# Filter spectrum computed behind the experts, input stage moved ahead of it, three early value chunks, query stacks issued from ScalarE

## The reference

```python
x = x + xattn0(layernorm(x), ctx)          # 16 heads, 1601 keys
x = x + ffn0(layernorm(x))                 # 8 experts, top 2 of each token
x = x + xattn1(layernorm(x), ctx, ...)     # top-32 attention, film, s4d, MLP
x = x + ffn1(layernorm(x))                 # attention with gated values

def s4d(x, ...):                           # inside xattn1
    powers = jnp.exp(dtA[:, :, None] * jnp.arange(L))
    K = 2.0 * jnp.einsum('dn,dnl->dl', dC, powers).real
    Kf = jnp.fft.rfft(K, n=n, axis=-1)     # the filter's spectrum: once
    xf = jnp.fft.rfft(x, n=n, axis=1)
    y = jnp.fft.irfft(xf * Kf.T[None], n=n, axis=1)[:, :L]
    return y + x * D_skip
```

## Time and profile before

| | |
|---|---|
| Median of 3 runs | 2865.64 us (2865.42 to 2866.55) |
| The profiled execution's own time | 2862.61 us |
| Its span | 2860.8 us |
| TensorE busy | 2277.7 us (80%) |
| VectorE, ScalarE, GpSimd busy | 1464.1, 1456.8, 917.3 us |
| Mean granted TensorE clock | 0.895 of 2.4 GHz |

### The profile page before, as it was taken

One profiled execution on the slowest core, in us unless ns is written; L12 is line 12 of the kernel. 1 busy time (PEld: TensorE's weight loads), 2 busy tenths in 40 slices (PEclk: granted clock), 3 DMA queues, 4 the chain that ended last, 5 costly groups with the idle time before them and its releaser, 6 DMA issues.

```text
span 2860.8 us, 36683 instructions
## 1 busy us (share of the span) xinstructions
PE 2277.7 (80%) x12668; PEld 1291.2 (45%) x12668; DVE 1464.1 (51%) x4388; ACT 1456.8 (51%) x2266; POOL 917.3 (32%) x473
## 2 busy tenths in 40 slices
PE   0567799999984899667899767899668898768997
PEld 0433222323222566336555446556446555446555
DVE  8756111121213111397575696574696564795563
ACT  2134477777771122384267582266582366681374
POOL 2023100101011111374058273076372085370094
PEclk9988899999996999858999868999768999769999
DMA  2044834443224111202113203013203023103022
GB/s 63 0 145 167 175 49 83 56 83 51 54 92 146 47 45 41 60 1 67 56 31 48 60 1 121 1 40 50 49 1 122 0 44 50 38 1 114 0 31 45
DMA packets 176516, 166.51 MB, mean 58 GB/s; under 512 B 84048, under 2 KB 147152, under 8 KB 176304
## 3 DMA queue, kind: packets, MB, share of 16 engines
q1 hardware_dynamic: 168816, 154.73, 23.2%
q0 software_dynamic: 7504, 9.35, 1.7%
HBM read 131.88 MB, written 32.32 MB: 57 GB/s over the span
## 4 chain that ended last, share of the span: by engine, by line
PE 45%; DVE 23%; POOL 11%; issue 8%; ACT 7%; DMA 4%; SPq 2%; DVEq 1%; POOLq 0%; another core or an unknown queue 0%; ACTq 0%
DVE sb_xnT L2358 5%; PE ps L1311 5%; POOL sb_arena L730 5%; PE ps L1322 5%; POOL sb_xtn L728 4%; ACT sb_arena L962 3%; PE ps L1493 2%; PE ps L1717 2%; PE ps L1665 2%; PE ps L1596 2%; PE ps L1506 2%; PE ps L1512 2%; PE ps L1735 2%; PE ps L1645 2%; PE ps L1654 2%
## 5 line engine op out<-in xcount | busy, mean ns | idle before, releaser
L962 ACT ACTIVATE sb_arena<-ps 128x1024 f32<-128x1024 f32 x416 | 402.7, 1021 | 121.2 <-PE ps L1311 115.1
L2358 DVE MAX8 sb_xnT<-sb_arena 128x8 f32<-128x60 f32 (+1 forms) x1728 | 246.8, 206 | 34.4 <-ACT sb_arena L1061 34.4
L2519 DVE TENSOR_REDUCE sb_arena<-ps 128x2 f32<-128x1024 f32 x128 | 156.2, 1223 | 203.3 <-PE ps L1735 203.0
L1311 PE MATMUL ps<-sb_arena 96*128 96x512 bf16 x832 | 234.8, 387 | 28.3 <-ACT sb_arena L962 14.3
L1564 PE MATMUL ps<-sb_arena,sb_xnT 32*128 32x400 f32 (+1 forms) x512 | 161.1, 715 | 111.6 <-ACT sb_arena L1061 107.7
L851 POOL TENSOR_TENSOR sb_arena<-sb_arena 128x1601 f32<-128x1601 f32 x56 | 176.5, 3152 | 161.6 <-DVE sb_arena L2346 158.1
L1322 PE MATMUL ps<-sb_arena 128*32 128x512 f32 x1664 | 225.1, 613 | 1.5 <-ACT sb_arena L962 1.5
L730 POOL TENSOR_TENSOR sb_arena<-sb_arena,sb_xtn 128x1024 f32<-128x1024 f32 (+1 forms) x112 | 208.4, 1861 | 8.8
L786 POOL DMA_INDIRECT taken_rows<-sb_taken,sb_slots x32 | 31.3, 977 | 547.9 <-DVEq L2116 539.3
L1146 ACT ACTIVATE sb_arena<-ps 128x512 f32<-128x512 f32 x256 | 151.9, 593 | 90.4 <-PE ps L1703 90.0
L728 POOL TENSOR_TENSOR sb_arena<-sb_arena 128x1024 f32<-128x1024 f32 (+1 forms) x16 | 24.1, 1506 | 533.6 <-DVEq L2476 528.3
(11 more groups left out here) (350 smaller groups left out, 4539.3 us busy)
## 6 DMA issues: line engine op xcount, KB each, us to landing
sb_arena<-k_spill SPq DMA_DIRECT2D x96, 208.0 KB, 8.1
sb_arena<-in_ctxT SPq DMA_DIRECT2D x12, 1601.0 KB, 7.3
sb_arena<-in_dft SPq DMA_DIRECT2D x5, 2048.0 KB, 7.6
k_spill<-sb_arena SPq DMA_DIRECT2D x12, 832.0 KB, 5.2
sb_arena<-in_w SPq DMA_DIRECT2D x16, 512.0 KB, 6.2
sb_arena<-in_idft SPq DMA_DIRECT2D x4, 2048.0 KB, 8.7
sb_arena<-in_wf SPq DMA_DIRECT2D x8, 1024.0 KB, 12.0
o_rows<-sb_arena SPq DMA_DIRECT2D x32, 256.0 KB, 2.3
```

The costliest lines, as they stand in the source:

```text
L962: A(probs0[:, 2 * (m % 4):2 * (m % 4) + 2, :], ps[:, 2 * (m % 2):2 * (m % 2) + 2, :], ACT.Exp).then_inc(pair_probs, 1)
L1311: ins = mm(ps[:, 2 * (m % 2) + i, :], k_stack[0:NSPLIT, h, k * P:(k + 1) * P], q_stack[0:NSPLIT, h, :], start=True, stop=True)
L2358: ins = V.max(cand[:, n % 2, 8 * j:8 * j + 8], s_sb[:, n % 6, c0:c0 + w])
```

## The change

- The spectrum's 32 products leave the set-up. They stand on TensorE behind the four key items of batch 0 in the third block, wait for a new load of the table (`dft_k`, 2 MB, issued by SyncE behind the experts' last store), and write PSUM banks 0 to 3. ScalarE evicts them into `k_cos` and `k_sin`; VectorE's three fix-ups follow behind its second layer norm there. `k_time` lies in the place of `k_cos` until then.
- `setup_done` is gone. The context is loaded right behind the first tokens. SyncE's three weight loads wait for the set-up products (`setup_p`), GpSimd's pads and TensorE's first key products for `setup_v` 9, which is the end of the copies into `k_time`.
- VectorE normalises the first tokens between the two halves of the copies.
- `EARLY_VALUES` is 3 instead of 5.
- ScalarE issues the query stacks of groups 0 and 1 behind the barrier; SyncE issues the key stacks, and all stacks of groups 2 and 3.

```diff
-        EARLY_VALUES = 5
+        EARLY_VALUES = 3
...
-        dft_s = at(o, [SEQ // P, 2 * SEQ]); o += SEQ // P * 2 * SEQ
-        s_e = at(o, [NPW])
-        k_time = at(o, [SEQ // P, DIM]); o += NPW
+        s_e = at(o, [NPW]); o += NPW
+        k_time = k_cos
+        dft_k = at(4096, [SEQ // P, 2 * SEQ])
...
 @block.sync
-            const(dft_s[:, :, :], a["dft"].rearrange("(c p) f -> p c f", p=P))
...
-            sp.wait_ge(setup_done, 1)
             sp.dma_start(ctxT[:, :, :], a["ctxT"][0].rearrange("(c p) k -> p c k", p=P)).then_inc(in_ctx, 16)
+            sp.wait_ge(setup_p, 2)
             sp.dma_start(wq0[:, :, :], a["wq0"].rearrange("(c p) n -> p c n", p=P)).then_inc(in_w, 16)
...
             for g in range(4):
-                stacks(0, g)
+                key_stacks(sp, 0, g)
+                if g >= 2:
+                    query_stacks(sp, 0, g)
...
+            sp.dma_start(dft_k[:, :, :], a["dft"].rearrange("(c p) f -> p c f", p=P)).then_inc(dft_k_loaded, 16)
             sp.wait_ge(batch_ended, 4)
...
 @block.gpsimd
-            pool.wait_ge(setup_done, 1)
+            pool.wait_ge(setup_v, 9)
...
 @block.scalar
             close_input(act)
+            for g in range(2):
+                query_stacks(nc.scalar, 0, g)
...
                 for n, (c0, w) in enumerate(COLS):
+                    if n == 2 and b == 0:
+                        act.wait_ge(spectrum_done, 1)
+                        half = FCH // 2
+                        spec_k = ps[:, 0:4, :].rearrange("p b (j d) -> p (b j) d", d=DIM)
+                        A(k_cos[:, :, :], spec_k[:, 0:half, :], ACT.Copy)
+                        A(k_sin[:, :, :], spec_k[:, half:FCH, :], ACT.Copy)
+                        act.drain().then_inc(spectrum_ready, 1)
                     if n == (1 if b else 2):
                         deviation()
...
 @block.tensor
-            pe.wait_ge(setup_v, 9)
-            for j in range(FCH):
-                for c in range(SEQ // P):
-                    ins = mm(ps[:, 2 + j // 2, (j % 2) * DIM:(j % 2 + 1) * DIM], dft_s[:, c, j * P:(j + 1) * P], k_time[:, c, :],
-                             start=(c == 0), stop=(c == SEQ // P - 1))
-            ins.then_inc(setup_p, 1)
-            pe.wait_ge(setup_done, 1)
...
                 pe.wait_ge(in_ctx, 16 * b + 16)
+                pe.wait_ge(setup_v, 9)
...
                 for n in range(len(COLS)):
                     context_item(b, n)
+                if b == 0:
+                    pe.wait_ge(dft_k_loaded, 16)
+                    for j in range(FCH):
+                        for c in range(SEQ // P):
+                            ins = mm(ps[:, j // 2, (j % 2) * DIM:(j % 2 + 1) * DIM], dft_k[:, c, j * P:(j + 1) * P], k_time[:, c, :],
+                                     start=(c == 0), stop=(c == SEQ // P - 1))
+                    ins.then_inc(spectrum_done, 1)
                 turn(b, xt, xn_ready, 0)
...
 @block.vector
+                dve.wait_ge(setup_p, 1)
+                time_rows(1)
+                dve.sem_inc(in_xn, 1)
+                in_tokens(1)
+                dve.wait_ge(setup_p, 2)
+                time_rows(0)
                 done(9)
-                dve.wait_ge(setup_p, 3)
...
```

More of the change, by code:

```diff
@@ L388, in program @@
         late_loaded = once("late_loaded")
+        dft_k_loaded = once("dft_k_loaded")
+        spectrum_done = once("spectrum_done")
+        spectrum_ready = once("spectrum_ready")
         film_scaled = once("film_scaled")
@@ L526, in program, with key_stacks, query_stacks @@
         block = ctx.enter_context(nc.Block())
+        def key_stacks(eng, b, g):
+            hs, rows = slice(4 * g, 4 * g + 4), slice(4 * g * D0, (4 * g + 4) * D0)
+            for i, part in enumerate(SPLIT_K):
+                eng.dma_start(k_stack[i * D0:(i + 1) * D0, hs, :],
+                              k_spill[b, part, rows].rearrange("(h d) k -> d h k", d=D0)).then_inc(stacked[g], 16)
+        def query_stacks(eng, b, g):
+            hs, rows = slice(4 * g, 4 * g + 4), slice(4 * g * D0, (4 * g + 4) * D0)
+            for i, part in enumerate(SPLIT_Q):
+                eng.dma_start(q_stack[i * D0:(i + 1) * D0, hs, :],
+                              q_spill[b, part, rows].rearrange("(h d) k -> d h k", d=D0)).then_inc(stacked[g], 16)
         @block.sync
@@ L596, in _ @@
             sp.sem_inc(sems_cleared, 1)
-            def stacks(b, g):
-                hs = slice(4 * g, 4 * g + 4)
-                rows = slice(4 * g * D0, (4 * g + 4) * D0)
-                for i, part in enumerate(SPLIT_K):
-                    sp.dma_start(k_stack[i * D0:(i + 1) * D0, hs, :],
-                                 k_spill[b, part, rows].rearrange("(h d) k -> d h k", d=D0)).then_inc(stacked[g], 16)
-                for i, part in enumerate(SPLIT_Q):
-                    sp.dma_start(q_stack[i * D0:(i + 1) * D0, hs, :],
-                                 q_spill[b, part, rows].rearrange("(h d) k -> d h k", d=D0)).then_inc(stacked[g], 16)
             def expert(e):
@@ L630, in _ @@
                     if b + 1 < NBATCH:
-                        stacks(b + 1, g)
+                        key_stacks(sp, b + 1, g)
+                        query_stacks(sp, b + 1, g)
                     else:
@@ L1165, in _ @@
             mm, tr = nc.tensor.matmul, nc.tensor.transpose
+            pe.sem_inc(in_k_done, 1)
+            pe.sem_inc(in_xT_done, 1)
+            pe.sem_inc(in_norms_done, 1)
             for n, part in enumerate((1, 0)):
@@ L1885, in setup_program, with time_rows @@
                 blocks = ps[:, :, :].rearrange("p k (g d a) -> p (k g) d a", d=4, a=LA)
-                for n, part in enumerate((1, 0)):
-                    dve.wait_ge(setup_p, n + 1)
+                def time_rows(part):
                     gs = slice(part * DIM // 8, (part + 1) * DIM // 8)
@@ L1892, in setup_program @@
                                                 blocks[LB * d:LB * (d + 1), gs, d, j::4])
[L1893 to L1905 removed]
+                    link(ins)
+                dve.wait_ge(setup_p, 1)
[4 more added lines that the diff above has]
+                time_rows(0)
+                done(9)
             IN_STEPS = 5
@@ L2317, in _ @@
                 layernorm(xn, xt, in_normal)
+                if b == 0:
+                    dve.wait_ge(spectrum_ready, 1)
+                    link(V.tensor_copy(k_cos0[:, :], k_cos[:, 0, :]))
+                    link(V.tensor_copy(k_cos0[0:1, :], k_sin[0:1, 0, :]))
+                    link(V.memset(k_sin[0:1, 0, :], 0.0))
                 def settle(n):
```

22 lines of the change are left out of this document (5 added, 17 removed).

## The result

The changed kernel takes 2840.93 us (median of 5 runs, 2824.65 to 2843.72) against 2865.64 (2864.42 to 2867.64) for the kernel before: a ratio of 0.9903 (95% interval 0.9886 to 0.992), a gain of 24.7 us where 41.6 were forecast. 2840.93 lies outside the forecast range of 2816 to 2837.

A forecast was written before the change was run, and what follows sets the result against it. The prediction took chains of work and waits in three stretches (set-up and input, the barrier, behind the experts) as the bound; 34.6 + 1 + 2.2 + 3 + 1.8 - 1 = 41.6 us gave 2824 us, range 2816 to 2837.

The forecast's parts named there:

- the input stage: Set-up to key products: with the spectrum moved away, key products start at 134.9 instead of 169.50, gaining 34.6 us.
- the table out of the first loads: Start of set-up: without the 2 MB table the phase load lands sooner, gaining 1 us (between 0 and 2).
- late weights: Rival, input stage: weights late again and clock low, 27.1 us gained instead of 34.6, total 2831.5; chance 0.12.
- slower: Rival, behind the experts: spectrum ends some 40 us later and its loss exceeds the other terms, 42.6 us; chance 0.03.
- three value chunks: Ahead of the barrier: three chunks instead of five at the low clock open it 2.2 us sooner.
- Query stacks on ScalarE: Behind the barrier: a second issuer lets attention start sooner, at 317.6, gaining 3 us (between 0 and 5.4).
- Clock at the start of attention: First attention: a shorter pause keeps TensorE at the high clock, gaining 1.8 us (bound 0).
- There is room for both at once: Behind the barrier: DMA can carry query and key stacks together, from 233 GB/s at 319 to 320 us.
- the second queue brings nothing: Rival, start of attention: terms of 3 and 1.8 us fall away, total 2828.8; chance 0.16.
- the spectrum behind the experts: Between key items and transposes: the moved spectrum loses 1 us, between a gain of 1.6 and a loss of 4.9.
- Square root 2.3 us late: Behind the experts: spectrum copies and table load delay ScalarE's root to 1180.7 instead of 1178.44, 2.3 us.
- the 3.9 us of clock that were to come back: Behind the experts: TensorE pauses 4.4 us instead of 18.9, so a still high clock returns 3.9 us.

The follow-up runs named there:

- e11: Changed kernel with ScalarE's root and key copies ahead of the two spectrum copies, query stacks still by ScalarE: 2838.71 us, ratio 0.9888.
- e10: e7 again without any edit: 2836.13 us, ratio 0.988.
- e2: Changed kernel with all stacks issued by SyncE again: 2835.55 us, ratio 0.9884.
- e4: Kernel before with only three early value chunks and the query stacks of groups 0 and 1 by ScalarE: 2863.33 us, ratio 0.9995.
- e8: Changed kernel with only group 0's query stacks by ScalarE, group 1's back on SyncE: 2833.99 us, ratio 0.9898.
- after: The changed kernel in its first runs, profiled execution 2824.65 us: median 2840.93 us, ratio 0.9903.
- e1: Changed kernel again without any edit: 2835.84 us, ratio 0.9898.
- e5: Changed kernel with the spectrum's load, products and two copies left out, a constant filled in instead: 2836.74 us, ratio 0.9895.
- e3: Changed kernel with five early value chunks instead of three: 2832.25 us, ratio 0.9895.
- e7: Changed kernel with all stacks by SyncE and ScalarE's root and key copies ahead of the spectrum copies: 2827.73 us, ratio 0.9866.
- e12: e9 with group 0's query stacks issued by ScalarE, all twelve loads with rows of 1 KB: 2831.07 us, ratio 0.9878.
- e14: e12 with SyncE holding every later stack until the last value chunk is evicted: 2819.58 us, ratio 0.9839.
- e9: e7 with group 0's key stacks in two pieces, 512 columns ahead of the queries, the rest behind: 2827.97 us, ratio 0.9843.
- e15: e9 again without any edit: 2823.29 us, ratio 0.9854.
- e13: Kernel before with three early chunks and group 0's key stacks split, all issued by SyncE: 2855.48 us, ratio 0.9966.

## Why the prediction was wrong

*Right: the input stage.* Key products 34.0 us sooner. Forecast were 34.6 and 1, together 35.6. The set-up itself ended 2.2 us sooner (the copies start at 125.55 instead of 127.76), since the phase load landed at 10.6 instead of 12.8 us: the table out of the first loads brought more than its 1 us. From there to the key products it takes 10.0 us instead of 7.2: the third weight load landed 4.8 us behind the set-up products, not 4.0, and the query products took 5.39 us, not 3.25, since the clock was still low. Two errors, 1.2 us to the good and 2.8 to the bad, mostly cancel; that the total fits so well is partly luck. The four passes kept their length: the first values start 33.9 us sooner, 33.3 on average in the thirteen kernels with the new input stage. Of the rival "late weights" the low clock came and the 7.1 us did not (the load took 3.6); "slower" did not occur.

*Mis-sized, to the good: three value chunks.* Forecast 2.2. From the first value chunk to the barrier it takes 7.8 us before, and 3.2 to 5.7, on average 4.4, in the twelve kernels with three chunks and the new input stage: a gain of 3.4. Where the three chunks ran at the low clock (5.5 us, as in e11) the gain is 2.1, near the forecast 2.2; in six of the twelve they ran in 2.85 us, at the high one.

*The step that failed: "Query stacks on ScalarE", with "Clock at the start of attention".* "There is room for both at once" rested on one window of 1 us with 233 GB/s. In windows of 2 us the engines are full from 2 us behind the barrier in every kernel with whole key stacks, at a share of 0.98 to 1.19 (one window of e10 has 0.81) and 108 to 188 GB/s. What sets the start is volume: six loads of 208 KB and six of 64 KB, 1.63 MB, take some 13 us (125 GB/s), and in no kernel that changes only the issuer (e2, e4, e8) is it less. Two issuers also lose SyncE's order: key stacks of the next group come in between. In the five kernels after, e1, e5, e8 and e11 attention started 18.5 us behind the barrier on average, where 12.7 was forecast, and at the low clock. Terms of 3 and 1.8 became -2.8 and 0: 7.6 us of the shortfall. The rival "the second queue brings nothing" (2828.8) was right in its mechanism, and still too kind, since it counted no loss. The rule from the Trainium skill that the prediction weighed ("DMA: Bandwidth & Descriptors", Issuing engines are not separate DMA queues) agrees with e2, e4 and e8; what the trace adds is that the second issuer cost 2.5 us (18.6 against 16.1).

A second part of that loss may be the instruction fetch. By the landings of the last query stack and the end of the q8 fetch, attention starts 0.1 us behind the stacks in before, e2, e3, e7, e10 and after (285.9, start 286.1), and 1.7 to 2.0 us behind the fetch in e1 (288.03), e4 (323.20), e5 (287.69), e8 (285.82) and e11 (288.41), where the stacks had landed 0.7 to 1.6 us earlier. In after the start lies 1.9 us behind a fetch too, so there the two are not told apart. That the fetch can decide rests on e12 and e14; for the others it is read from these distances.

*Mis-sized: the spectrum behind the experts.* Forecast -1, with -4.9 as the worst. Load and products came as forecast (after: the products start 8.5 us behind the item and take 14.08; forecast 8.3 and 14.3). From item to MAX8 there are 41.1 us before and 45.0, 48.6, 45.0, 41.5 and 47.4 in the five kernels with the copies ahead of the root (after, e1, e2, e3, e8): 45.5 on average, -4.4. "Square root 2.3 us late" was a good mean (0.5, 3.7, 2.1, 1.7, 3.5 late: 2.3), but the 3.9 us of clock that were to come back did not: TensorE fell to 0.50 some 27 us behind the item and stayed there for 14 to 17 us in four of the five. With the root first (e7, e9 to e12, e14, e15) it is 41.6 on average. The kernel before, e4, e5 and e13, with no spectrum there, have 42.5; against these four the term is -3.0. So on average root first removes the term. What it removes for certain is the root's delay, 2.3 us; the rest goes with the stretches at the low clock, and the groups overlap (37.7 to 44.8 with the root first, 41.5 to 48.6 without). In the time alone neither e10 nor e11 shows it.

*The sum.* For the profiled pair before and e1, from the table: 36.3 to the barrier, -3.5, +3.4, -7.5, -2.0 make 26.7 us (2860.8 less 2834.1). With the averages: 33.3 + 3.4 - 2.8 - 4.4 = 29.5, against 29.4 measured in e1 and 24.7 in the first runs. So of the 41.6 forecast 7.6 us are missing at the start of attention, 3.4 behind the experts and 2.3 in the input stage and its table, and 1.2 came on top from the chunks. *What stays open:* the unchanged columns vary together between 2491.5 (after) and 2512.5 (e11), 21 us. On average they make 2495.1 in the three kernels with the old input stage (before, e4, e13) and 2500.8 in the thirteen with the new one. The forecast handed each gain on in full; whether these 5.7 us are a cost of the change or spread is not shown. The mean granted clock lay between 0.899 (after) and 0.891 (e10, 2512.0), but also at 0.891 in e13 with 2496.1; why one execution gets more low-clock stretches than another was not settled.

## What to carry to other kernels

Before giving loads to a second issuer, read the DMA share over several microseconds. Where it stood at 1.0 here, a second issuer started the consumer no sooner and fewer bytes ahead of it did, so split the transfer by what is needed first (here 6 us at the start, and 8.2 us in the time, e9 against e10). Put an eviction that nobody waits for behind the small instruction on which the next engine waits, and look where in the program order a table load comes to stand. And cut every profile at the same instructions: local distances told what the times alone could not.

## What was not expected of the hardware

- An instruction fetch (16 KB, q8, taken to be TensorE's) comes late when the DMA engines are full of data: 11.9 us behind the barrier in e12, 5.9 in e9 and 6.7 in e14. In e12 the first product followed its end by 1.9 us, 5.9 us behind the last stack. A wait that the profile puts down to "issue" can be this.
- Stacks with rows of 1 KB held the DMA engines at 0.44 to 0.64 for 130 to 145 GB/s (e9, one issuer, 274 to 278 us); whole key stacks (rows of 3.3 KB) at 0.97 to 1.10 for 115 to 130 (e7 and e1, 274 to 280 us). With two issuers the small loads too went to 1.08, at 176 GB/s (e14, 272 to 274 us).
- Executions of one kernel differ by up to 19 us (changed kernel, 2824.65 to 2843.72), and those of the kernel before by up to 13 within one run (2858.32 to 2871.43), where the first three had lain within 1.1.
